# Two-layer perceiver block on one core: head pairs in one tile, projection begun tile by tile, context products four steps behind the scores

## The reference, cut to what matters

```
q = norm(x) @ W_q;  k = ctx @ W_k;  v = ctx @ W_v          # 16 heads of 64
attn = softmax(q k^T / 8 + mask)                           # 64 x 6272 for each head
x = x + concat_heads(attn @ v) @ W_o
```

## Time and profile before

| what | value |
|---|---|
| median of three runs | 461.99 us |
| the profiled execution: its time | 457.64 us |
| its span, first to last instruction | 455.8 us |
| PE busy | 408.1 us, 90% of the span |
| DVE, ACT, POOL busy | 347.3, 280.3, 221.4 us |
| layer 1's 56 steps, from the first score to the last context product | 21.8 to 176.9 us |
| layer 2's 56 steps | 223.4 to 370.9 us |
| mean granted TensorE clock | 0.984 |

### The profile page before, as it was taken

How to read it: one execution, slowest core, us unless ns; L and a number is a source line. 1 busy time by engine, 2 the same in 40 slices (tenths; PEclk the granted TensorE clock), 3 DMA queues, 4 the chain that set the end, 5 groups by cost and what they waited for, 6 DMA issues and landing times.

```text
span 455.8 us, 11595 instructions
## 1 busy us (share of the span) xinstructions
PE 408.1 (90%) x4541; PEld 326.4 (72%) x4541; DVE 347.3 (76%) x943; ACT 280.3 (61%) x540; POOL 221.4 (49%) x141
## 2 busy tenths in 40 slices
PE   7788999999999989989878998999999899983776
PEld 7646777777777778889656776777767789752675
DVE  3778878888888886546699989898887874388653
ACT  3367888888788861344187997998997611260120
POOL 1359889888765600010015697976565000169210
PEclk9999999999999999999999999999999999995989
DMA  8899797989899989300059999999999700000000
GB/s 323 237 236 197 136 173 137 177 176 214 183 227 236 166 192 424 134 1 4 1 94 197 186 177 201 164 175 202 211 166 194 151 2 1 1 0 1 1 0 4
DMA packets 185894, 64.97 MB, mean 143 GB/s; under 512 B 181280, under 2 KB 181488, under 8 KB 185072
## 3 DMA queue, kind: packets, MB, share of 16 engines
q1 hardware_dynamic: 185552, 63.18, 70.2%
q10 hardware_dynamic: 288, 1.05, 0.7%
HBM read 18.76 MB, written 0.03 MB: 41 GB/s over the span
## 4 chain that ended last, share of the span: by engine, by line
PE 39%; DVE 28%; issue 9%; DMA 8%; POOL 7%; ACT 7%; SPq 2%; DVEq 0%; POOLq 0%; ACTq 0%
PE ps L477 12%; DVE probs L561 11%; PE ps L445 10%; DMA probsT<-halves 5%; PE ps L695 5%; ACT probs L505 3%; DMA moe<-in_ctxT 2%; ACT halves L512 2%; DVE U L579 2%; DVE probsT L594 2%; PE ps L457 2%; POOL moe L1220 2%; PE ps L952 2%; DVE den L574 1%; POOL moe L1215 1%
## 5 line engine op out<-in xcount | busy, mean ns | idle before, releaser
L537 POOL TENSOR_TENSOR halves<-probs,halves 128x896 f16<-128x896 f32 x67 | 126.6, 1893 | 82.0 <-ACT halves L512 81.1
L445 PE MATMUL ps<-ctxT_parts,GT_parts 128*128 128x512 f16 (+1 forms) x672 | 145.4, 353 | 13.8 <-DVE negmax L561 11.7
L477 PE MATMUL ps<-ctxN,probsT 128*128 128x128 f16 x2352 | 148.7, 219 | 2.8 <-DMA probsT<-halves 1.7
L477 PEld LDWEIGHTS ps<-ctxN,probsT 128*128 128x128 f16 x2352 | 139.6, 98 | 15.6 <-issue 2.5
L505 ACT ACTIVATE probs<-probs,shifted 128x896 f32<-128x896 f32 x112 | 115.5, 1031 | 14.0 <-DVE shifted L566 14.0
L445 PEld LDWEIGHTS ps<-ctxT_parts,GT_parts 128*128 128x128 f16 x672 | 60.1, 98 | 66.4 <-DVE negmax L561 16.9
L512 ACT CAST halves<-probs 128x896 f16<-128x896 f32 x92 | 84.9, 923 | 0.1
L561 DVE CUSTOM_DVE_ANT_0 probs<-ps,zero,negmax 128x896 f32<-128x896 f32 x56 | 67.5, 1204 | 1.4 <-PE ps L445 1.3
L561 DVE CUSTOM_DVE_ANT_0 probs<-ps,maskb,negmax 128x896 f32<-128x896 f32 x56 | 67.4, 1204 | 1.2 <-POOL halves L537 0.7
L695 PE MATMUL ps<-cst 128*128 128x128 f32 x490 | 65.8, 283 | 0.0
L695 PEld LDWEIGHTS ps<-cst 128*128 128x128 f32 x490 | 61.0, 197 | 3.2 <-issue 2.1
(11 more groups left out here) (347 smaller groups left out, 381.4 us busy)
## 6 DMA issues: line engine op xcount, KB each, us to landing
moe<-in_ctxT SPq DMA_DIRECT2D x7, 448.0 KB, 8.3
moe<-in_mask SPq DMA_DIRECT2D x12, 224.0 KB, 5.3
moe<-in_gateT SPq DMA_DIRECT2D x2, 1024.0 KB, 9.3
moe<-in_upT SPq DMA_DIRECT2D x2, 1024.0 KB, 10.8
moe<-in_downT SPq DMA_DIRECT2D x2, 1024.0 KB, 12.8
probsT<-halves SPq DMA_TRANSPOSE x92, 4.6
wv<-in_wv SPq DMA_DIRECT2D x2, 512.0 KB, 4.1
wo<-in_wo SPq DMA_DIRECT2D x2, 512.0 KB, 5.0
```

Source lines behind the costliest of these rows:

```text
L445: ins = pe.matmul(ps[:, 2 * b + h, 0:width], GT_parts[:, g_part, r * P:(r + 1) * P], ctxT_parts[:, keys:keys + width], start=(g_part == 0 ...
L477: ins = pe.matmul(ps[:, bank, 0:D], probsT_parts[:, b, p_part, k * P:(k + 1) * P], ctxN_parts[:, at:at + D], start=(p_part == 0 and c_part ...
L537: eng.tensor_tensor(halves_of(L, n)[:, 1, :], probs[:, n % BUFS, :], halves_of(L, n)[:, 0, :], ALU.subtract).then_inc(lower_of(L, n)[0], 1)
```

## The change

It has eight parts.

1. `PV_LAG` 5 to 4 and `ADD_LAG` 6 to 5: `pv(n)` stands behind `score(n + 6)`.
2. Step 0 of both layers is turned on PE. Step 1 of layer 1 gets its lower part from DVE where POOL made it. ACT's upper part of step 0 and DVE's lower part of step 0 go.
3. At a layer's end the turn of step 53 moves behind `pv(51)`, next to that of step 54.
4. Tiles hold head pairs (2j, 2j + 1). `fold_q_pe` writes the queries' products in that order; in layer 1 PE waits once for its own earlier matmuls there.
5. DVE makes only the reciprocals (`invert`); ACT scales the tiles (`scale` in `turn_u_act`). PE turns tiles 0 to 3 before the last context product, 4 to 6 behind it, and tile 7 after the first half of the W_v products. ACT copies tiles 0 to 3 and 4 to 6, DVE tile 7.
6. `project_pe` begins W_v products with tiles 0 to 3; its `stay_warm(6, 4)` and `stay_warm(6, 1)` go, in the third call too.
7. The mask has 128 rows in memory (the 64 rows twice); a chunk is one DMA of 128 rows. Four chunks are loaded ahead of the first context turn, three and the parameters behind it.
8. PE's first 12 matmuls take 512 float16 columns where they took 128 float32 ones; `stay_warm(6, 8)` in the fold of layer 1 becomes 5.

```diff
-PV_LAG, ADD_LAG = 5, 6
+PV_LAG, ADD_LAG = 4, 5
-            return L == 0 and n % 4 == 3 or n >= STEPS - 3 or n == STEPS - 5
+            return L == 0 and n % 4 == 3 or n >= STEPS - 3 or n in (0, STEPS - 5)
...
-                return n in (0, 2) or 4 <= n < 30 and n % 4 == 1 or n == STEPS - 4
+                return n in (1, 2) or 4 <= n < 30 and n % 4 == 1 or n == STEPS - 4
...
-                for a in range(2):
-                    sp.dma_start(mask_raw(c)[a * S:(a + 1) * S, :],
-                                 dram["mask"][:, c * CK:(c + 1) * CK]).then_inc(sem(f"ld_mask{c}"), 16)
+                sp.dma_start(mask_raw(c), dram["mask"][:, c * CK:(c + 1) * CK]).then_inc(sem(f"ld_mask{c}"), 16)
...
             for i in range(STEPS + PV_LAG):
                 if i + 2 < STEPS:
                     score(i + 2)
-                if 1 <= i < STEPS - 1 and on_pe(L, i - 1):
+                if 1 <= i < STEPS - 2 and on_pe(L, i - 1):
                     turn(i - 1)
+                if i == STEPS + PV_LAG - 1:
+                    turn_u_pe(pe, L, range(0, 4))
                 if i >= PV_LAG:
                     pv(i - PV_LAG)
                 else:
                     stay_warm(pe, 7, 2)
-                if STEPS - 1 <= i <= STEPS and on_pe(L, i - 1):
+                if i == STEPS - 1:
+                    turn(i - 2)
+                if STEPS - 1 <= i <= STEPS:
                     turn(i - 1)
...
-            def scale(r):
+            def invert(r):
                 dve.wait_ge(sem("den_added"), base + (CH - 1) * RT + r + 1)
                 dve.reciprocal(rden[:, r:r + 1], den[:, r:r + 1]).then_inc(sem("den_inverted"), 1)
-                dve.wait_ge(sem("u_added"), base + (CH - 1) * RT + r + 1)
-                dve.wait_ge(sem("den_inverted"), L * RT + r + 1)
-                dve.tensor_scalar(U[:, r, :], U[:, r, :], rden[:, r:r + 1], None, ALU.mult).then_inc(
-                    sem("u_scaled"), 1)
...
-            stay_warm(pe, 6, 4)
-            pe.wait_ge(sem("ut_copied"), 2 * i + 2)
+
             for j in range(PAIRS):
+                if i == 2:
+                    if j == 0:
+                        pe.wait_ge(sem("ut_copied"), 2 * i + 2)
+                elif j == 0 or j == 4:
+                    pe.wait_ge(sem("ut_copied"), 2 * i + 1 + j // 4)
+                elif j == RT - 1:
+                    pe.wait_ge(sem("ut_last"), i + 1)
                 for par_ in range(2):
-                    h, g = 2 * j + par_, par_ * PAIRS + j
+                    h = 2 * j + par_
                     ins = pe.matmul(ps[par_ * DK:(par_ + 1) * DK, 2 - j // 4, j % 4 * S:(j % 4 + 1) * S],
-                                    wv[:, h * DK:(h + 1) * DK], UT[:, g // 2, (g % 2) * S:(g % 2 + 1) * S],
+                                    wv[:, h * DK:(h + 1) * DK], UT[:, j, par_ * S:(par_ + 1) * S],
                                     start=True, stop=True)
                 if j % (PAIRS // 2) == PAIRS // 2 - 1:
                     ins.then_inc(sem("o_ready"), 1)
-            stay_warm(pe, 6, 1)
+                if i < 2 and j == 3:
+                    turn_u_pe(pe, L, (RT - 1,))
...
+            for r in range(RT - 2):
+                scale(r)
             act.wait_ge(sem("ch_back"), 1)
-            act.activation(ut, src, ACT.Copy, scale=u_back[:]).then_inc(sem("ut_copied"), 1)
+            copy(0, 0, 4)
+            scale(RT - 2)
+            scale(RT - 1)
+            copy(1, 4, RT - 1)
```

More of the change, by code:

```diff
@@ L402, in _ @@
                 sp.dma_start(ctxT_raw[:, keys], dram["ctxT"][:, keys]).then_inc(sem(f"ld_ctxT{c}"), 16)
-            load_mask(0)
-            load_mask(1)
+            for c in range(4):
+                load_mask(c)
+            turn_ctx(0)
+            for c in range(4, CH):
+                load_mask(c)
             load("par", par[:], "par")
-            turn_ctx(0)
-            for c in range(2, CH):
-                load_mask(c)
             for n in range(STEPS):
@@ L526, in flash_act @@
                     exps(i)
-                if i == 0:
-                    upper(0)
-                if 2 <= i <= STEPS and not on_pe(L, i - 1):
+                if 1 <= i <= STEPS and not on_pe(L, i - 1):
                     upper(i - 1)
@@ L601, in flash_dve @@
                     aside[i]()
-                if i == 1:
-                    lower(dve, L, 0)
-                if 3 <= i < STEPS + 2 and on_vector(L, i - 2) and not on_pe(L, i - 2):
+                if 2 <= i < STEPS + 2 and on_vector(L, i - 2) and not on_pe(L, i - 2):
                     lower(dve, L, i - 2)
@@ L713, in fold_q_pe @@
                 pe.wait_ge(sem("q_copied"), 2)
-                for j in range(PAIRS):
-                    for par_ in range(2):
-                        rows = slice(par_ * DK, (par_ + 1) * DK)
-                        ins = pe.matmul(ps[:, 4 + par_, j * S:(j + 1) * S], wkT[rows, j, :], QT[rows, j, :],
-                                        start=True, stop=True)
+                for swap in range(2):
+                    for k in range(PAIRS // 2):
+                        for par_ in range(2):
+                            rows, half = slice(par_ * DK, (par_ + 1) * DK), par_ ^ swap
+                            j, col = 4 * half + k, k * P + par_ * S
+                            ins = pe.matmul(ps[:, 4 + half, col:col + S], wkT[rows, j, :], QT[rows, j, :],
+                                            start=True, stop=True)
+                            if swap == 0 and k == PAIRS // 2 - 1:
+                                ins.then_inc(sem("q_ready"), 1)
+                    if swap == 0:
+                        pe.wait_ge(sem("q_ready"), 3)
                 ins.then_inc(sem("g_ready"), 2)
-                stay_warm(pe, 6, 8)
+                stay_warm(pe, 6, 5)
                 pe.wait_ge(sem("squares"), 2)
@@ L724, in fold_q_pe @@
                 return
-            for par_ in range(2):
-                for j in range(PAIRS):
-                    for side in range(2):
-                        rows = slice(side * S, (side + 1) * S)
-                        ins = pe.matmul(ps[rows, 4 + par_, j * S:(j + 1) * S], w_qk[par_][:, j, rows], src[:, 0:S],
-                                        start=True, stop=True)
+            for half in range(2):
+                for k in range(PAIRS // 2):
+                    for par_ in range(2):
+                        for side in range(2):
+                            rows, col = slice(side * S, (side + 1) * S), k * P + par_ * S
+                            ins = pe.matmul(ps[rows, 4 + half, col:col + S], w_qk[par_][:, 4 * half + k, rows],
+                                            src[:, 0:S], start=True, stop=True)
                 ins.then_inc(sem("g_ready"), 1)
@@ L886, in _ @@
             for _ in range(12):
-                pe.matmul(ps[:, 6, 0:P], U[:, 0, :], U[:, 0, :], start=True, stop=True)
+                pe.matmul(ps[:, 6, :], U[:, 0, :].bitcast(F16)[:, 0:P],
+                          U[:].rearrange("p r d -> p (r d)").bitcast(F16)[:, 0:4 * P], start=True, stop=True)
             loaded(pe, "cst", "in0")
@@ L894, in _ @@
             flash_pe(pe, 0)
-            turn_u_pe(pe, 0)
+            turn_u_pe(pe, 0, range(4, RT - 1))
             loaded(pe, "out0")
@@ L988, in _ @@
             flash_pe(pe, 1)
-            turn_u_pe(pe, 1)
+            turn_u_pe(pe, 1, range(4, RT - 1))
             loaded(pe, "out1")
```

48 lines of the change are left out of this document (26 added, 22 removed).

## The result

The changed kernel takes 466.21 us in the median of 11 runs (462.56 to 468.35), the kernel before 461.48 (457.48 to 463.44) beside it. The ratio is 1.0115, with a 95% interval of 1.0074 to 1.0156: slower, by over one per cent. The time lies in my range (458.0 to 467.5), but on the side that I gave 0.30, and next to rival 2 (467.3), not the forecast (462.7).

A forecast was written before the change was run, and what follows sets the result against it. A nearly full PE (busy 90%) bounds the kernel, with SP's transpose queue level late in layer 2. Lag +7.3, layer ends -6.8, first steps +0.4, third projection -0.2: +0.7 on 461.99 gives 462.7 us; range 458.0 to 467.5.

The forecast's parts named there:

- rival 2: Layer 2, steps 9 to 47: the loop from score to context product closes, +5.3 us, 467.3 us; chance 0.23.
- The ends of the layers: Last score to end of projection, each layer: 3.4 us shorter, 6.8 us in all (bounds 5.4 to 8.4).
- rival 4: Layer ends: ACT holds the scalings behind its last copies, gain 1.5 instead of 3.4 us a layer; 466.5 us; chance 0.05.
- The third projection: Behind layer 2: the third projection loses its four idle matmuls, -0.2 us.
- The lag: Step loops at lag four: PE waits for late transposes, +3.3 us in layer 1, +4.0 in layer 2 (bounds +4.8, +10.9).
- the first steps: Start of each layer's loop: a wait for a maximum goes, other work delays maxima; +0.2 us a layer, +0.4 in all.
- five loops of 1.3 us: Ceiling for layer 2, steps 9 to 47: a late transpose returns seven steps later, five times, 6.5 us.
- The floor: Step loops, if transposes land when they do now: last score 2.2 us later in layer 1, 2.6 in layer 2.
- the loop of "seven steps": Step loops: a stalled PE delays scores, which feed the transpose seven steps later, late again if its own landing is slow.
- Rival 1: Step loops: the transposes recover and the floor holds, -3.5 us, 458.5 us; chance 0.28.
- Rival 3: Step loops: new waits lower PE's clock once in each layer, 5 us lost each time, 472.7 us; chance 0.04.
- The estimate from the page on DMA: Step loops: at 261 GB/s a transpose takes 1.8 us, under a step's 2.3, so transposes would never queue.

The follow-up runs named there:

- e2: The kernel before with PV_LAG 4 and ADD_LAG 5 and nothing else of the change; ratio 1.0205 to the kernel before.
- e8: The changed kernel with PV_LAG 5, ADD_LAG 6 and step 0 turned by a DMA again; median 459.85 us, ratio 0.9967 to the kernel before.
- e1: The changed kernel with PV_LAG back at 5 and ADD_LAG at 6; median 456.63 us, ratio 0.9919 to the kernel before.

## Why the prediction was right or wrong

The number fell inside the range, and that was in part luck: the range was wide enough for most of rival 2, whose mechanism is what happened, while the forecast was worked out from another one.

**The ends of the layers** were right: -3.5 and -3.7 where -3.4 stood. The stretch from the end of the last context product to the end of the projection is 4.37 in the kernels with the early projection and 6.1 in the others (e2), so rival 4 is out.

**The third projection** was right (-0.2). The rest is near: 0.6 us ahead of and between the loops, where the fourteen profiles spread from 21.8 to 26.5 and from 40.5 to 42.7. The tail's 2.1 us, forecast at nothing, are the clock: PE, 20 us from 20 us behind the third projection on, before and after.

```profile
413.40:433.40 20.00, 12.76 (x82) 9.90 (x82) 15.05 (x55) 2.93 (x5) 10.46 (x6) 0.81 0.00 1
```

```profile
418.00:438.00 20.00, 14.99 (x82) 12.34 (x82) 15.07 (x55) 2.51 (x4) 10.52 (x6) 0.68 0.00 1
```

The same 82 matmuls take 2.2 us more of PE, as the mean lies nearer to the lower of the two levels of the earlier trace rows. The tail is 64.5 to 69.1 us in all these profiles, whatever the kernel, so I take these 2.1 us for chance of the two profiles. It fits that the profiles' spans differ by 6.7 us and the medians by 4.7 only.

**The lag** was wrong in size, and it decided the sign: +7.3 stood there, bounded by 10.9, and the middle of the loops cost 11.7 (4.5 + 7.0, plus the 0.2 that the first steps gave). The waits came near where I put them (from steps 33 and 11 on), from step 28 on in layer 1 and from step 8 on in layer 2, but where I had five loops of 1.3 us in layer 2, 19 of the 43 transposes of steps 8 to 50 landed last before their product (three before the change), and nine of them left PE idle, for 8.2 us together. What failed is the weighing under rival 2. I wrote that the loop closes when score to landing exceeds 15.0 us, and held "landings of 5.0 in the median" against it. That is one link, not the sum. The sum could be read from the same trace. Step 24 of layer 2 in the kernel before, first its score in time, then its transpose by its line (issued at 291.10, landing at 295.56):

```profile
280.00 1.31 PE L445 MATMUL ps<-ctxT_parts,GT_parts 128*128 128x512 f16 x6 [0.95 <-DVE negmax L561]
```

```profile
L397 SPq DMA_TRANSPOSE probsT<-halves x1: 3132/3132/3132, 291.1 to 291.1; - x1
...
DMA to landing us min/median/max: 4.5/4.5/4.5
```

That is 15.6 us, and all 43 transposes of steps 8 to 50 lie over 15.0 (15.1 the least, 16.8 the median). By my own criterion rival 2 was the forecast. Worked out as a loop: 15.3 us against the 13.9 of six steps, 1.4 lost in each six, is up to 10 us over 43 steps; with the 14.6 of the changed kernel, where SP's queue holds back 9 transposes and not 27, it is 5. These are estimates from medians; layer 2 lost 7.0.

The floor failed for the same reason, though it was used as a bound only: "late by landing minus place" counts each slow transpose once, whereas lateness returns with every turn when the ring has no room left. And the loop of "seven steps" was too long. It went by PE alone. Over the add on VectorE lateness reaches the maximum six steps on, and, as the upper part stands behind the next exp, the transpose five steps on (from 315.21 to 328.15 above).

**Rival 1** is out: transposes did recover, to 4.4 us, and it didn't help, because a ring's other links stay. **Rival 3** is out: the clock stood at 1.00 in both stretches shown above, and in both loops as a whole. The estimate from the page on DMA changed nothing of this. (Of it the prediction says "the second rival below"; it means rival 1.)

**The first steps** were mis-sized: +0.4 forecast, -0.2 measured, and e8 puts the turn of step 0 on PE at a gain of 1.4 us or more at lag five.

Open: the mask's order, the regrouped folds and the other first matmuls of PE were not tried alone. Whether the add alone could stay six steps behind, which would give the ring one step more room, was not tried either.

## What to carry over

When a pipeline's lag is shortened, sum the whole ring from the trace, through every in-order queue that it passes (here VectorE's add ahead of a later maximum, and ScalarE's exp ahead of the upper part of the step before), and compare it with lag times pace; one link against one step says nothing. If the sum is over the room, a lateness comes back turn after turn, and not the slow transfers alone pay. When a link is shortened, look at what its instruction now runs beside: an order that is good for one queue can make two engines stand in each other's way (here 2.65 us where 1.08 would do).

## What was not expected of the hardware

- VectorE's tile of 128x896 from two SBUF operands takes 1.08 us, and 2.65 when it starts 0.18 us behind GpSimd's like operation of 1.89, which is not slowed.
- A DMA transpose with half the bytes lands in 2.9 us in place of 4.4. If the rest goes with the bytes, some 1.4 us are the same for both, an estimate.
- The slow landings come together with the fetching of instructions. Of the changed kernel's 17 landings over 5.5 us, all had a packet of an instruction queue (8 KB or more) start while they were in flight, of its 73 others 35; over all fourteen profiles it is 248 of 253 against 446 of 1013. That the one causes the other was not tried.
- The granted clock also differs in the loads at the start, at equal work: over the first 26 us it was 0.93 in the changed kernel and 0.74 in e1, which differ in the lags alone. The same 32 matmuls (L712) took 2.53 and 4.04 us, and the first score came at 21.9 and 26.0.

```profile
0.00:26.00 26.00, 20.93 (x132) 14.73 (x133) 14.87 (x37) 8.37 (x14) 8.90 (x20) 0.93 0.84 303
...
14.04 2.53 PE L712 MATMUL ps<-OT,wkT 64*128 64x64 f32 x32
```

```profile
0.00:26.00 26.00, 20.25 (x111) 16.79 (x111) 11.16 (x28) 7.23 (x12) 5.00 (x17) 0.74 0.67 257
...
15.56 4.04 PE L712 MATMUL ps<-OT,wkT 64*128 64x64 f32 x32
```
